# Moving the later norms' transposes from TensorE to VectorE block turns and a DRAM scratch

## The reference

```python
def ffn(x):                      # widths 128 -> 512 -> 512 -> 512 -> 128
    h = silu(tlin(x, w1_w, w1_s)) * tlin(x, w2_w, w2_s)
    h = gelu(tlin(h, h1_w, h1_s))          # exact gelu
    h = gelu(tlin(h, h2_w, h2_s))
    return tlin(h, w3_w, w3_s)             # tlin(x, w, s) = (x @ w.T) * s, w in {-1, 0, 1}

def attn(x):
    h = layer_norm(x, gamma, beta)
    keys, values = h @ Wk.T + bk, h @ Wv.T + bv
    kw = exp((keys @ Wka.T + bka) / sqrt(128))
    kw = kw / cumsum(kw, axis=1)
    return cumsum(kw * keys, axis=1) * values

x = x + 0.5 * ffn(layernorm(x))
x = x + attn(layernorm(x))
x = x + 0.5 * ffn(layernorm(x))
```

## Time and profile before

| | value |
|---|---|
| median of 3 runs | 376.88 us (376.24 to 377.13) |
| span of the profiled execution, first to last instruction | 374.9 us |
| what lies around the span (median less span) | 1.98 us |
| PE busy | 368.0 us, 98% |
| DVE busy | 321.9 us, 86% |
| ACT busy | 314.1 us, 84% |
| POOL busy | 52.6 us, 14% |

### The profile page before, as it was taken

How to read it: one execution, slowest core, us unless ns; L and a number is a source line. 1 busy time by engine, 2 the same in 40 slices (tenths; PEclk the granted TensorE clock), 3 DMA queues, 4 the chain that set the end, 5 groups by cost and what they waited for, 6 DMA issues and landing times.

```text
span 374.9 us, 5278 instructions
## 1 busy us (share of the span) xinstructions
PE 368.0 (98%) x1662; PEld 291.9 (78%) x1662; DVE 321.9 (86%) x713; ACT 314.1 (84%) x549; POOL 52.6 (14%) x67
## 2 busy tenths in 40 slices
PE   7999999999999999999999999999999999999996
PEld 2678888787787877778788787778877778788885
DVE  5898787999999799999988999989799999976733
ACT  4999699989977999798699979967998998686763
POOL 3531101202101202201021120102101210020000
PEclk9999999999999999999999999999999999999999
DMA  7760000000000000000000000000000000000001
GB/s 246 277 265 1 2 0 0 1 2 1 0 2 0 1 2 2 2 0 1 2 0 1 2 1 28 2 28 1 2 29 0 0 30 1 30 1 28 2 0 58
DMA packets 4494, 9.81 MB, mean 26 GB/s; under 512 B 625, under 2 KB 1905, under 8 KB 4209
## 3 DMA queue, kind: packets, MB, share of 16 engines
q1 hardware_dynamic: 3744, 8.65, 6.3%
q10 hardware_dynamic: 720, 0.80, 0.6%
HBM read 7.35 MB, written 2.10 MB: 25 GB/s over the span
## 4 chain that ended last, share of the span: by engine, by line
PE 95%; DMA 2%; DVE 1%; SPq 1%; issue 0%; ACT 0%; ACTq 0%
PE hid_ps L449 60%; PE gate_ps L449 8%; PE y_ps L449 7%; PE up_ps L449 7%; PE xt_ps L462 3%; DMA x_sb<-x 2%; PE y_ps L462 2%; PE xt_ps L632 2%; PE xt_ps L629 2%; PE xt_ps L635 2%; PE up_ps L507 1%; PE gate_ps L507 1%; DVE gate L855 0%; PE xt_ps L449 0%; DVE xt_sb L924 0%
## 5 line engine op out<-in xcount | busy, mean ns | idle before, releaser
L449 PE MATMUL hid_ps<-act_hi,hi_h 128*128 128x512 f32 x480 | 195.6, 408 | 0.0
L449 PE MATMUL hid_ps<-act_lo,hi_h 128*128 128x512 f32 x480 | 186.8, 389 | 0.0
L877 DVE TENSOR_TENSOR act_lo<-full,act_hi 128x512 fp32r<-128x512 f32 x185 | 122.2, 683 | 26.8 <-ACT act_hi L708 24.3
L701 ACT ACTIVATE full<-hid_ps,vec 128x512 f32<-128x512 f32 x123 | 84.4, 686 | 34.9 <-PE hid_ps L449 31.2
L449 PEld LDWEIGHTS hid_ps<-act_hi,hi_h 128*128 128x128 f32 x480 | 90.1, 188 | 22.4 <-issue 4.1
L449 PEld LDWEIGHTS hid_ps<-act_lo,hi_h 128*128 128x128 f32 x480 | 90.2, 188 | 22.1 <-issue 4.3
L708 ACT ACTIVATE act_hi<-full 128x512 fp32r<-128x512 f32 x127 | 78.5, 630 | 2.3
L362 POOL TENSOR_TENSOR rstd<-veps,half 128x4 f32<-128x4 f32 x24 | 35.2, 1467 | 272.5 <-DVE veps L840 272.5
L855 DVE SCALAR_TENSOR_TENSOR gate<-tanh,gate_ps 128x512 f32<-128x512 f32 x60 | 40.6, 679 | 9.2 <-ACT tanh L684 8.6
L684 ACT ACTIVATE tanh<-gate_ps,s_half 128x512 f32<-128x512 f32 x60 | 40.8, 686 | 8.2 <-PE gate_ps L449 8.2
L867 DVE SCALAR_TENSOR_TENSOR full<-up_ps,s_half,gate 128x512 f32<-128x512 f32 x60 | 44.2, 742 | 0.9
(11 more groups left out here) (159 smaller groups left out, 397.8 us busy)
## 6 DMA issues: line engine op xcount, KB each, us to landing
xt_sb<-xt SPq DMA_DIRECT2D x1, 2048.0 KB, 10.9
out<-xt_sb SPq DMA_DIRECT2D x7, 256.0 KB, 2.0
x_sb<-x SPq DMA_DIRECT2D x1, 1536.0 KB, 6.6
raw_h<-h2t SPq DMA_DIRECT2D x4, 256.0 KB, 7.3
raw_h<-h1t SPq DMA_DIRECT2D x2, 256.0 KB, 5.9
raw_w<-w2t ACTq DMA_DIRECT2D x1, 256.0 KB, 4.0
raw_w<-w1t SPq DMA_DIRECT2D x1, 256.0 KB, 3.8
raw_h<-h1t ACTq DMA_DIRECT2D x1, 256.0 KB, 6.7
```

Of the source, the lines that this page charges most:

```text
L449: mm = eng.matmul(ps, w, a, start=(first and n == 0), stop=(last and n == len(seq_) - 1))
L701: eng.activation(full23[m % 2][:, :], home23(n, T, m)[:, :], ACT.Gelu, scale=col("sh1" if n == 2 else "sh2", m)).then_inc(s_gelu[n], 1)
L877: eng.tensor_tensor(act_lo[a][:, m, :], full[m % 2][:, :], act_hi[a][:, m, :].bitcast(F32), ALU.subtract).then_inc(s_lo[n], 1)
```

## The change

All norms but the first three (`BY_PE`) lose their PE transposes of `z`: 21 of 24, namely feed-forward tiles 3 to 15 and all attention tiles. In their place DVE transposes each 32x32 block of `z` into `zt_b` (one instruction of 128x512), SP writes that to a DRAM scratch `turns` (256 KB), waits until it has landed, and reads it back with the blocks rearranged, by four transfers into 32 partitions each, in runs of 32 floats (128 bytes). ACT and DVE then read `xnt_b` in SBUF instead of `xt_ps` in PSUM. Both scratch buffers are used in turns (`slot`).

From norm 3 on, `bn_aggr` and `veps` leave DVE. POOL computes the same from the raw `bn_stats` output with seven small operations (`aggregate`), ahead of its power.

The orders are written out, one string for each of 16 steps and each engine, SP and POOL too. `ORDER`, `FIRST_STEP`, `LAST_STEP` and the items `zwait` are gone; the waits of `zwait` now stand at the head of `z`. SP's steps are shown whole, those of the other engines for steps 7 and 8 alone.

```diff
+STEPS = {
+    "SP": (
+        "",
+        "turn",
+        "a0:turn turn",
+        "a1:turn turn",
+        "turn",
+        "a2:turn turn",
+        "a3:turn turn",
+        "turn",
+        "a4:turn turn",
+        "a5:turn store turn",
+        "store turn",
+        "a6:turn store turn",
+        "a7:turn store turn",
+        "store turn",
+        "store",
+        "store",
+    ),
...
     "PE": (
...
+        "p2.0 p4 p2.1 u p2.2 p1.0 p1.1 a3:values p2.3 a4:u p1.2 p1.3 p3.0 p3.1 p3.2 p3.3",
+        "p1.0 p1.1 p2.0 p4 p2.1 u a4:logits p2.2 a4:keys p2.3 p1.2 a5:u a4:values p1.3 p3.0 p3.1 p3.2 p3.3",
...
     "ACT": (
...
+        "gelu2.0 a3:keys high2.0 t gelu2.1 high2.1 tanh.0 gelu2.2 tanh.1 z gelu2.3 high2.2 high1.0 high2.3 "
+        "tanh.2 tanh.3 high1.1 gelu3.0 a4:z high3.0 gelu3.1 high1.2 9:t high3.1 gelu3.2 high1.3 9:tanh.0 "
+        "high3.2 9:tanh.1 gelu3.3 high3.3",
...
     "DVE": (
...
+        "dt a3:recip.1 stats t low2.0 low2.1 a3:weight gate.0 up.0 gate.1 turn up.1 a4:stats low2.2 low2.3 "
+        "low1.0 gate.2 up.2 gate.3 a3:weight_keys a4:turn low1.1 low3.0 up.3 9:t a3:pool low3.1 low1.2 low1.3 "
+        "low3.2 a3:values low3.3",
+        "a3:dt gate.0 dt up.0 gate.1 stats low2.0 a4:cumsum up.1 a4:recip.0 low2.1 turn a4:recip.1 a5:stats "
+        "low2.2 low2.3 gate.2 low1.0 low1.1 gate.3 up.2 up.3 a5:turn low3.0 10:t a4:weight low3.1 low1.2 "
+        "a4:weight_keys low1.3 low3.2 a4:pool low3.3",
...
+BY_PE = (0, 1, 2)
+AGGREGATE = 3
...
+            def turn(kind, t):
+                i, use = slot(kind, t)
+                eng.wait_ge(s_turn, turn_of[kind, t] + 1)
+                if use > 0:
+                    eng.wait_ge(s_turned[i], 64 * use)
+                eng.dma_start(turns[i], zt_b[i][:, :]).then_inc(s_parked[i], 16)
+                if use > 0:
+                    before, at = by_dma[turn_of[kind, t] - 2]
+                    eng.wait_ge(*((s_xlo, at) if before == "ffn" else (s_ht, at + 1)))
+                eng.wait_ge(s_parked[i], 16 * (use + 1))
+                blocks = turns[i].rearrange("(s c) (j q r) -> q c j s r", c=32, j=SUB, r=32)
+                for b in range(4):
+                    eng.dma_start(xnt_b[i][32 * b:32 * b + 32, :].rearrange("c (j s r) -> c j s r", j=SUB, r=32),
+                                  blocks[b]).then_inc(s_turned[i], 16)
...
+            def aggregate(n):
+                stats, done = stats_b[n % 2], 6 * (n - AGGREGATE)
+                a, b = (1.0 + EPS, EPS * EPS) if n in att_norms else (1.0, EPS)
+                eng.wait_ge(s_bn, SUB * n + SUB)
+                eng.tensor_tensor(pair_diff[:, :], stats[:, :, 1], stats[:, :, 4], ALU.subtract).then_inc(s_agg, 1)
+                eng.tensor_tensor(pair_sum[:, :, :], stats[:, :, 1:3], stats[:, :, 4:6], ALU.add).then_inc(s_agg, 1)
+                eng.wait_ge(s_agg, done + 1)
+                eng.tensor_tensor(diff_sq[:, :], pair_diff[:, :], pair_diff[:, :], ALU.mult).then_inc(s_agg, 1)
+                eng.wait_ge(s_agg, done + 2)
+                eng.tensor_scalar(var_part[:, :], pair_sum[:, :, 1], a / P, b, ALU.mult, ALU.add).then_inc(s_agg, 1)
+                eng.wait_ge(s_agg, done + 3)
+                eng.tensor_scalar(diff_part[:, :], diff_sq[:, :], a / 4.0, None, ALU.mult).then_inc(s_agg, 1)
+                eng.tensor_scalar(neg_mean[:, :], pair_sum[:, :, 0], -0.5, None, ALU.mult).then_inc(s_agg, 1)
+                eng.wait_ge(s_agg, done + 5)
+                eng.tensor_tensor(veps[:, :], var_part[:, :], diff_part[:, :], ALU.add).then_inc(s_ve, 1)
+                eng.wait_ge(s_agg, done + 6)
...
+                elif stage == "t" and t not in BY_PE:
+                    i, use = slot("ffn", t)
+                    eng.wait_ge(s_p1, MC * t)
+                    eng.wait_ge(s_turned[i], 64 * (use + 1))
+                    eng.activation(xn_hi[:, :], xnt_b[i][:, :], ACT.Copy).then_inc(s_xhi, 1)
...
+                elif stage in ("turn", "att_turn"):
+                    kind = "ffn" if stage == "turn" else "att"
+                    i, use = slot(kind, t)
+                    eng.wait_ge(s_za, norm_of[kind, t] + 2)
+                    if use > 0:
+                        eng.wait_ge(s_parked[i], 16 * use)
+                    eng.transpose(zt_b[i][:, :], z[:, :]).then_inc(s_turn, 1)
```

More of the change, by code:

```diff
@@ L49 @@
 )
-FIRST_STEP = {
[6 rows of a table removed]
-}
-ORDER = {
[5 rows of a table removed]
+STEPS = {
[17 more added lines that the diff above has]
+    ),
+    "POOL": (
+        "norm",
+        "norm",
+        "a0:norm norm",
+        "a1:norm norm",
+        "norm",
+        "a2:norm norm",
+        "a3:norm norm",
+        "norm",
+        "a4:norm norm",
+        "a5:norm norm",
+        "norm",
+        "a6:norm norm",
+        "a7:norm norm",
+        "norm",
+        "",
+        "",
+    ),
[17 rows of a table added]
     ),
     "ACT": (
[10 rows of a table removed]
[44 rows of a table added]
     ),
     "DVE": (
-        "a:stats low2.0 a:aggr t a:veps low2.1 gate.0 up.0 gate.1 up.1 low2.2 gate.2 low1.0 low2.3 dt up.2 low1.1 "
-        "stats gate.3 aggr up.3 veps a:cumsum low3.0 a:recip.0 low1.2 low3.1 low1.3 low3.2 a:recip.1 low3.3",
-        "b:stats a:weight b:aggr t b:veps a:weight_keys low2.0 a:pool gate.0 a:values gate.1 low2.1 a:dt up.0 up.1 "
[6 rows of a table removed]
-    ),
-}
[L90 to L95, removed]
[40 rows of a table added]
+    ),
+}
 POOL_FIRST = ("norm", 1, 2)
-AHEAD = {"stats": 2, "aggr": 2, "veps": 2, "norm": 2, "zwait": 2, "z": 2, "t": 1, "p1": 1, "tanh": 1, "gate": 1,
-         "up": 1, "high1": 1, "low1": 1, "u": 2, "p4": -1, "dt": -1}
+BY_PE = (0, 1, 2)
+AGGREGATE = 3
+AHEAD = {"stats": 2, "aggr": 2, "veps": 2, "norm": 2, "z": 2, "t": 1, "p1": 1, "tanh": 1, "gate": 1,
+         "up": 1, "high1": 1, "low1": 1, "u": 2, "turn": 2, "p4": -1, "dt": -1, "store": -1}
 def macaron_block(nc, x, xt, w1t, w2t, h1t, h2t, w3t, wkt, wkat, wvt, wkn, vecs, out, seq):
@@ L111, in macaron_block @@
     assert D == P and TOK % seq == 0
[L112 to L115, removed]
+    assert all(len(steps) == 2 * NT for steps in STEPS.values())
     with ExitStack() as ctx:
@@ L140, in macaron_block @@
         z = sb("z", [P, TOK])
+        zt_b = [sb(f"zt_{i}", [P, TOK]) for i in range(2)]
+        xnt_b = [sb(f"xnt_{i}", [P, TOK]) for i in range(2)]
+        turns = nc.dram_tensor("turns", [2, P, TOK], F32).ap()
         xn_hi = sb("xn_hi", [P, TOK], F32R)
@@ L267, in xt_tile, with items, slot @@
             return xt_sb[:, (t % NT) * TOK:(t % NT + 1) * TOK]
[L270 to L275, removed]
+        def items(order, i):
+            for item in order.split():
+                which, _, stage = item.rpartition(":")
+                stage, _, chunk = stage.partition(".")
+                chunk = int(chunk) if chunk else None
+                if which in ("hi", "bits", "flag", "vec"):
+                    yield which, chunk, stage
+                elif which == "last":
+                    yield "last_" + stage, chunk, 2 * NT - 1
+                elif which[:1] == "a":
+                    yield "att_" + stage, chunk, int(which[1:])
+                else:
+                    yield stage, chunk, int(which) if which else i + AHEAD.get(stage, 0)
+        norm_of = {("ffn", t): t for t in range(2)}
+        for i, order in enumerate(STEPS["DVE"]):
+            for stage, _, t in items(order, i):
+                if stage in ("stats", "att_stats"):
+                    norm_of["ffn" if stage == "stats" else "att", t] = len(norm_of)
+        assert len(norm_of) == 3 * NT
+        att_norms = {n for (kind, _), n in norm_of.items() if kind == "att"}
         turned = [sum(1 for k, m in norm_of.items() if m <= n and (k[0] == "att" or k[1] >= NT))
                   for n in range(len(norm_of))]
+        by_dma = [key for key in norm_of if key[0] == "att" or key[1] not in BY_PE]
+        pe_turns = [sum(1 for k, m in norm_of.items() if m <= n and k not in by_dma) for n in range(3 * NT)]
+        dma_turns = [sum(1 for k, m in norm_of.items() if m <= n and k in by_dma) for n in range(3 * NT)]
+        turn_of = {key: k for k, key in enumerate(by_dma)}
+        def slot(kind, t):
+            k = turn_of[kind, t]
+            return k % 2, k // 2
         def norm_blk(kind, t, j):
@@ L314, in macaron_block, with schedule, step @@
         block = ctx.enter_context(nc.Block())
+        def schedule(engine, emit, part):
+            def step(i, order):
+                for stage, chunk, t in items(order, i):
+                    emit(stage, chunk, t)
+            if part == "start":
+                step(-1 if engine == "PE" else -2, START[engine][0])
+            if part == "first":
+                step(-1, START[engine][1])
+            if part == "second":
+                step(0, SECOND_LAYER)
+            if part == "rest":
+                for i, order in enumerate(STEPS[engine]):
+                    step(i, order)
         @block.sync
```

(17 more changed lines are left out.)

74 lines of the change are left out of this document (45 added, 29 removed), and 115 rows, old and new, of tables (FIRST_STEP, ORDER, STEPS).

## The result

| | before | after |
|---|---|---|
| median of the runs timed together | 377.0 us (376.24 to 377.36, 4 runs) | 382.98 us (382.27 to 383.37, 4 runs) |
| span of the profiled execution | 374.9 us | 381.5 us |
| forecast | | 368.5 us (366.3 to 376.0) |

The account below looks back on a forecast made before the run. PE was taken as the bound, DVE as nearest follower. 376.88 us less 9.8 us of PE work gives 367.1, plus 1.4 us of turn waits reaching PE: 368.5 us, 8-in-10 range 366.3 to 376.0.

Parts of the forecast that it names:

- First latency: `stats` to turn: POOL's seven operations, rstd, nmr, ACT's z and handovers take 5.3 us against 4.2 us of DVE work in step 7.
- at most 14 us of DVE waiting: DVE's total stand at some 13 close block turns, against 20 us that DVE has free over steps 1 to 13.
- PE's saving: Removing 21 transpose groups from PE saves 9.8 us, between 9.3 and 10.3 us.
- my sum: 376.88 less 9.8 us gives 367.1 us if PE keeps its pace, before 1.4 us for turn waits reaching PE.
- DVE's balance: DVE loses aggr and veps, 0.43 us a norm, and gains a 0.60 us turn: +3.6 us in all, beside PE.
- The second latency: From turn to first reader, transpose, parking write, four reads and handovers take 6.3 us, leaving 1.4 us margin at the tightest.
- DVE becomes the pace: Turn waits 1.1 us late at 13 places; 6 us reach PE in steps 5 to 12: 373 us, chance 0.20.
- The small reads are slow: The 128-byte scratch reads land 6.4 us later, holding ACT and DVE at some 14 turns: 387 us, chance 0.12.
- The block turn is slow: DVE's 128x512 transpose takes 1.2 us, giving about 374 us, or 3.4 us, giving near 420; chance 0.04.
- PE's saving is eaten by new restarts: 9.8 us of new gaps on PE leave the time unchanged at 376.5 us; chance 0.04.
- The last line of the prediction: A POOL operation of 128x4 far above 0.3 us would be the step that fails first; no chance given.

Follow-up runs that it names:

- the last experiment: Kernel after with a stretch added behind its end: twelve 128x4 POOL operations beside fourteen DVE instructions of one kind, in five phases; POOL starts every 0.15 to 0.60 us.
- e2: Kernel after with POOL's seven operations cut to two, from the even half's statistics alone, leaving out part of the norm: 370.06 us, ratio to before 0.9831.
- e1: Kernel after with the pooling of the statistics back on DVE for every norm, each operation behind one further instruction: 373.86 us, ratio to before 0.9924.
- e3: Kernel after with the four scratch reads in plain 2 KB rows, blocks not rearranged: 382.39 us, ratio to before 1.0155.
- e13: e2 with two unused operations, difference and sum of the halves, put in front, so POOL's chain has four: 373.4 us, ratio to before 0.9906.
- e11: Kernel after with the pooling on DVE for all norms, directly behind the statistics: 375.72 us, ratio to before 0.9971.

## Why the prediction was wrong, step by step

**The step that failed** is "First latency: `stats` to turn", in two terms.

- *The size of the chain.* I took the seven at 0.26 us, `nmr`'s median, 1.8 us in all. Their means in the kernel after add up to 2.6 us, and in the norm shown above they span 2.7. The bounds (1.4 to 4.2) held it; the value taken was near the wrong end. `nmr` runs behind a long `rstd`, while `pair_diff` starts just as DVE leaves `stats` for a run of `low` with two SBUF inputs, and the last experiment shows what that costs. `rstd` came out shorter than I took it (1.04 us at the median against 1.38), which hid part of the error. The greatest `nmr` in the earlier trace rows, 0.60, was the same effect and could have been read as such; it stands beside four `act_lo` in a row in the kernel before:

```profile
191.41 2.49 DVE L877 TENSOR_TENSOR act_lo<-full,act_hi 128x512 fp32r<-128x512 f32 x4
...
191.55 0.60 POOL L364 TENSOR_TENSOR nmr<-neg_mean,rstd 128x4 f32<-128x4 f32 x1
```

- *Who waits.* I priced only DVE's stand at the turn, "at most 14 us of DVE waiting"; it was 17.6 us, a quarter more. But I let just 1.4 us of it reach PE. The chain's first waiter is ACT, at `z`: 15.8 us, with `gelu` and `high` behind it in its queue, and PE waits for `full`, the output of `gelu`, for 12.9 us at its weight loads and 6.2 at its matmuls. I had written down what stands behind the turn and not what stands behind `z`. Cutting the chain from seven operations to two took 12.9 us off the time, more than nine times the 1.4 us that I had allowed for the whole chain.

**What came as forecast, or near it.**
- PE's saving. Transposes into `xt_ps` fell from 90 to 6, and plain matmuls still start 0.2265 us apart between gaps. With most of the chain's waits gone (`e2`) the time is 370.1, against the 367.1 of my sum. So 6.7 of the 9.8 us are shown; the other 3 are not, and part of them is waits that are left.
- DVE's balance. I had +3.6 us; busy time rose from 321.9 to 326.0. I had taken 0.60 us for the turn from start to start; in the last experiment, back to back, it is 0.59. Its length is 0.71 us. The estimate that I had worked out from the Trainium skill's page "VectorE: DVE Perf Modes" ("The three transpose paths") was also 0.71; the 311 ns behind it are that page's figure for bf16, and this transpose is in float32.
- The second latency. The parking write lands in 2.0 us, the reads in 2.6 (I had said 2 to 2.5), and `xn_hi` and `h_t` wait for them for 2.4 us in all.

**The rivals.** "DVE becomes the pace" named the right place, late turns in steps 5 to 12, but the wrong carrier and price. It gave 373 us because it gave DVE's waits alone to PE; DVE was never the pace, and with 7.1 us more work on it (`e1`) the kernel is 9.1 us faster. "The small reads are slow" was my main case on the slower side and is refuted by the landings (2.6 us) and by `e3`: the time was slower, but not by this mechanism. The rule of the Trainium skill that I had set beside it ("DMA: Bandwidth & Descriptors", "Specifications": at least 512 B a transfer for line rate) did not decide here, since landings of 64 KB in 128-byte runs were 0.7 us longer and the time within 0.6 us of that with 2 KB rows. "The block turn is slow" and "PE's saving is eaten by new restarts" did not occur. The last line of the prediction, a 128x4 operation far above 0.3 us as the step to fail first, named what happened, with no price on it.

**What stays open.** `e2` is 3.0 us above my sum. Its page puts 1.6 us of idle time before PE's fast matmuls, where before has none; the turn waits for 3.4 us and `xn_hi` for 3.5. Whether the rest is a saving smaller than 9.8 I did not take apart. `e1` is another 3.8 us above `e2`, with 7.7 us more work on DVE. Its chain (3.6 us) is as long as that of `e13` (3.7), and so nearly is its time (373.9 and 373.4), so a late `nmr` may be most of it; but `e1` waits less for `nmr` and `z` than `e13` does (4.4 and 3.4 us against 5.8 and 8.1), and `e11` shows that a late `act_lo` has a share. How the 3.8 us divide is not shown. The best kernel that computes everything is `e1`: 373.86 us, 0.8% under before and 2.4% under after.

## What to carry to other kernels

Where small work moves to an idle engine, its load is not its price. Follow its result to the first instruction that waits for it, and list what stands behind that instruction in *its* queue, and behind the next waiter too. Price a small GpSimd operation by what VectorE runs beside it, and where its latency counts put instructions there that read PSUM, or the turn (the last experiment suggests this order; no kernel here tried it). Before moving a late reader further back, look for what closes the window from behind: here the reuse of a PSUM bank and a transfer's deadline left no room to move them all by even one item.

## What the runs showed of the hardware

- A 128x4 operation on GpSimd is 0.19 to 0.20 us long beside an idle VectorE, beside one that reads PSUM and beside the block turn. It is 0.65 beside one with two inputs from SBUF, and 0.38 beside a `tensor_scalar` of 128x512 with one. In the two held cases GpSimd gets through one operation per VectorE instruction. "SBUF — State Buffer" of the Trainium skill ("SBUF: two separate sides") says that VectorE and GpSimd share a pair of ports as an exclusive lock, taken by VectorE with two SBUF inputs or in its two-port modes; the run agrees in all five phases.
- That `tensor_scalar` with one SBUF input starts every 0.335 us, against 0.60 us for two inputs or a PSUM source.
- The 128x512 block turn in float32 is 0.67 to 0.71 us long, and 0.59 from start to start.
